# Spreading the routing scatters of a graph layer with eight experts over four steps each

## The chip, the cores and the metric

The kernel runs on one core of one Trainium2 chip. The metric is the device time of one execution in microseconds (us), the median of several runs. Lower is better.

## What is computed

One graph layer and one mixture-of-experts layer follow each other on 6250 nodes of 256 numbers each, in float32, with 100000 edges that are sorted by their target node.

```python
h = layernorm(x)
msg_sum = segment_sum(h[src], dst, N)                 # 100000 edges
agg = msg_sum / maximum(deg, 1)[:, None]
x = x + concatenate([h, agg], axis=1) @ W.T + b       # W is 256 x 512
xn = layernorm(layernorm(x)) * gamma + beta
top_vals, top_idx = top_k(xn @ Wr + br, 2)            # 8 experts, 2 for each node
w = softmax(top_vals)
y = sum over the 2 experts e of w_e * (gelu(xn @ W1[e] + b1[e]) @ W2[e] + b2[e])   # 256 -> 512 -> 256
out = x + y
```

## The kernel before

All engines run one common schedule of numbered steps t, each engine as its own instruction stream; nothing but semaphores ties the streams together. A line such as `if t == ...` in an engine's stream function puts work behind a step of that engine.

**Edge steps, t = 0 to 829.** A step sums 128 edges. GpSimd (POOL) gathers the 128 source rows from `h_rows` in HBM by an indirect DMA (L662). TensorE (PE) multiplies them with a one-hot matrix into a PSUM bank (L764), VectorE (DVE) adds the 257 columns to the node tile's sums in `acc` (L1125). The first 96 steps use 48 gathers twice over, so there are 782 gathers. From step 96 on gather and step go one to one. The gathered rows lie in a ring of `RING` = 17 places, so POOL may be up to 17 steps ahead: it waits for `summed` of step t - 17 (L660).

**Node tiles.** The 49 tiles of 128 nodes close one after another, about every 15 steps. Some steps after a tile has closed, its sums are scaled (ACT L580), transposed and multiplied with W (PE L770, L772, L777, L778), added to x and normalised (DVE L1135 on, ACT L604).

**Batches and routing.** Node tiles are routed in 12 batches (`SIZES = [6, 6, 6, 5, 5, 5, 4, 2, 5, 3, 1, 1]`, `FLUSH = 7`). For batch b the choice of experts is made at `CHOICE[b]`, the places in the experts' queues at `PLACES[b]` (DVE, up to L1040), and the list of expert tiles at `LISTS[b]`. From step `SCATTER[b]`, 17 steps after `PLACES[b]`, POOL scatters the normalised rows from `pay` into `queue` in HBM by 2 * size(b) indirect DMAs (L673), 12 for the first three batches, 10 for the next three, 8 for the seventh, one behind the gather of each step. `pay` and `place_i` have two halves, so batch b + 2 waits for the scatters of batch b (L601, L1039).

**Expert tiles.** 112 tiles of 128 queue rows are computed: SyncE (SP) fetches the rows 6 steps ahead (L540), for a batch's first tile after all scatters of the batch have landed (L533). PE transposes them (L845), ACT copies the expert's W1 into `w1_now` (L625) and the rows (L627), PE makes the hidden layer (L833), ACT the gelu (L633), PE the second product (L858), DVE adds the bias (L1183), and SP stores the result in `answers` (L546). `w1_now` exists once, so a copy waits for the hidden layer of the tile before (L623). The tiles' steps are laid out by hand:

```python
t = SCATTER[b] + 2 * size(b) + 7 if SCATTER[b] < STEPS else max(PLACES[b] + 8, STEPS + 5)
for j in range(UPTO[b], UPTO[b + 1]):
    if begin_at:
        t = max(t, begin_at[-1] + (PACE if begin_at[-1] + PACE < STEPS else 3))
    begin_at.append(STEPS if STEPS - CLEAR <= t < STEPS else t)
```

With `PACE = 7` a tile starts every 7 steps while edge steps run, and every 3 steps afterwards. The first four tiles (batch 0) start at steps 238 to 259, the tiles of batch 1 at 328 to 405, of batch 2 at 418 to 495; from there the tiles follow each other every 7 steps up to tile 74 at step 824. 37 tiles (75 to 111) start at step 830 or later.

**Tail, t = 830 to 976.** The remaining tiles, and `BACK`: each node tile's two answers per node are gathered from `answers` (POOL L685, two per node tile), weighted and added (DVE L1186, L1187) and stored (SP L550). The first 39 node tiles begin 4 steps after tile 84 is done, at step 868, one every two steps; the last 10 wait for the last tile.

Of the kernel before, what the change touches and what calls it, by code (L numbers as in the profile page):

```python
# [48 lines left out]
def build(nc, x, src, dst, gnn_w, gnn_b, gamma, beta, wr, br, w1, b1, w2, b2, out):  # L49
# [14 lines left out]
    STEPS = ET + NT - 1  # L64
# [37 lines left out]
    NB = len(BATCHES)  # L102
    FLUSH = 7
# [240 lines left out]
    def gathered(t):  # L344

        return t - SHARED if t >= BOTH else t // 2 if t % 2 == 0 else None

    def place_of(g):

        return early[:, g, :] if g < SHARED + EXTRA else grow[:, (g - SHARED - EXTRA) % RING, :]  # L350
# [14 lines left out]
    def size(b):  # L365
        return BATCHES[b][1] - BATCHES[b][0]
# [7 lines left out]
    PLACES = [t + 3 for t in CHOICE]  # L374
    LISTS = [t + 1 for t in PLACES]
    SCATTER = [t + AHEAD + 2 for t in PLACES]
    SCATTER = [t if t < STEPS else max(p + 1, STEPS) for t, p in zip(SCATTER, PLACES)]
    begin_at = []
    for b in range(NB):
        t = SCATTER[b] + 2 * size(b) + 7 if SCATTER[b] < STEPS else max(PLACES[b] + 8, STEPS + 5)  # L380
        for j in range(UPTO[b], UPTO[b + 1]):
            if begin_at:
                t = max(t, begin_at[-1] + (PACE if begin_at[-1] + PACE < STEPS else 3))
            begin_at.append(STEPS if STEPS - CLEAR <= t < STEPS else t)
# [12 lines left out]
    def backs(t):  # L397

        return [r for r in range(NT) if BACK[r] == t]

    def back(r, s):

        return grow[:, place_in_ring(STEPS - RING + 2 * (r % PAIRS) + s), 0:D]
# [4 lines left out]
    def answered(engine, j):  # L408

        if j >= 0:  # L410
            engine.wait_ge(s_answer, 16 * (j + 1))
# [239 lines left out]
    def gpsimd_stream():  # L651
        pool.wait_ge(s_hst, 16 * NLB)
        srcs_up.wait(pool)
        for t in range(END):
            g = gathered(t) if t < STEPS else None
            if g is not None:
                if g >= RING:
                    pool.wait_ge(got[g % RING], 16 * (g // RING))
                if g >= SHARED + EXTRA + RING:
                    summed.wait(pool, t - RING)  # L660
                cell_of = CELLS + g if g < SHARED else t
                pool.indirect_dma_start(place_of(g)[:, 0:D], None, h_rows,  # L662
                                        bass.IndirectOffsetOnAxis(srcs[:, cell_of:cell_of + 1], 0)).then_inc(got[g % RING], 16)
            for b in range(NB):
                for n in range(2 * size(b)):
                    if t == SCATTER[b] + n:
                        if n == 0:
                            place_up.wait(pool, b)
                            if b == FLUSH + 1:
                                pool.wait_ge(s_pad, 16 * (X + 1))  # L670
                            if b == NB - 1:
                                pool.wait_ge(s_pad, 16 * (2 * X + 1))
                        pool.indirect_dma_start(queue, bass.IndirectOffsetOnAxis(place_i[:, b % 2, n % 2, n // 2:n // 2 + 1], 0),  # L673
                                                pay[:, b % 2, n // 2, :], None).then_inc(s_sent[b], 16)
            for r in backs(t):
                if r == 0:
                    answered(pool, FIRST_TILES - 1)
                if r == CUT:
                    answered(pool, ALL_TILES - 1)
                if r < PAIRS:  # L680
                    summed.wait(pool, STEPS - RING + 2 * r + 1)
                whole_up.wait(pool, r - PAIRS)
                answer_up.wait(pool, r)
                for s in range(2):
                    pool.indirect_dma_start(back(r, s), None, answers[r >= CUT],  # L685
                                            bass.IndirectOffsetOnAxis(answer_i[:, s, r:r + 1], 0)).then_inc(s_pair[r % PAIRS], 16)
# [507 lines left out]
    sync_stream()  # L1194
    scalar_stream()
    gpsimd_stream()
    tensor_stream()
    vector_stream()
# [24 lines left out]
```

## Time and profile before

| | |
|---|---|
| median of 3 runs | 1425.81 us |
| runs | 1423.88 to 1431.27 us |
| profiled execution, first to last instruction | 1787.5 us |
| granted TensorE clock in it, mean | 0.842 of full |

The profiled execution is 361.7 us longer than the median; no time of its own beside this span is shown for it. The profile says for each engine when it ran an instruction, how long that took, and what ended the idle time before it: the name of a line is what wrote the semaphore, "issue" is time for which the profile shows no wait, and "remote" or "another core or an unknown queue" is a wait whose releaser isn't recorded. A semaphore update can come later than the modelled end of the matmul that sends it. Busy time is not the same as time on the path that sets the end.

### The profile page before, as it was taken

Reading aid. Unit: us, or ns where it says so; the run is one execution under the profiler, and the core shown is the slowest. Engines: PE = TensorE matmul, PEld = TensorE weight load, DVE = VectorE, ACT = ScalarE, POOL = GpSimd, SP = SyncE. Lnnn points to the kernel's source line nnn. Section 1 sums busy time; section 2 is a strip of 40 time slices with the busy share of each in tenths; the row PEclk is TensorE's granted clock in tenths of the full one; section 3 lists DMA queues with packets and bytes.
Section 4 is the critical chain, followed back from the end, with each engine's and each line's share of the span. In section 5 each row is a group of like instructions: output and inputs, shape, how many; then the busy total and the mean of one; then the engine's idle time right before and its main releaser. Section 6 shows DMA issues by size and latency. Waiting matters only on the chain.

```text
span 1787.5 us, 23229 instructions
## 1 busy us (share of the span) xinstructions
PE 1241.8 (69%) x5751; PEld 942.1 (53%) x5751; DVE 812.6 (45%) x2587; ACT 463.2 (26%) x1019; POOL 948.0 (53%) x995
## 2 busy tenths in 40 slices
PE   3223777765874778678787688688788868795881
PEld 2101343442652556556566566566666656684771
DVE  8312663452444445344434444445366565642333
ACT  4200000210220134124124224233322413463440
POOL 3574035666556655655655655665556565115544
PEclk9855998777886889898888889888889889997886
DMA  9732044433333333343333333343344333324553
GB/s 335 247 104 64 1 153 151 133 99 100 110 99 94 107 111 106 115 121 95 113 111 101 110 112 104 109 122 101 115 128 120 105 109 107 101 78 132 160 159 119
DMA packets 128488, 212.63 MB, mean 119 GB/s; under 512 B 25378, under 2 KB 94295, under 8 KB 128119
## 3 DMA queue, kind: packets, MB, share of 16 engines
q0 software_dynamic: 48352, 129.18, 25.2%
q1 hardware_dynamic: 77561, 81.17, 13.7%
q8 instruction: 52, 0.85, 0.2%
q10 hardware_dynamic: 2446, 0.80, 0.2%
q14 instruction: 77, 0.63, 0.1%
HBM read 167.37 MB, written 50.87 MB: 122 GB/s over the span
## 4 chain that ended last, share of the span: by engine, by line
PE 44%; another core or an unknown queue 17%; issue 16%; DVE 11%; ACT 6%; DVEq 2%; DMA 2%; POOL 1%; ACTq 0%; POOLq 0%
PE psum L764 16%; PE psum L833 9%; PE psum L858 8%; DVE acc L1125 5%; PE psum L777 4%; ACT expert_buf L633 2%; PE psum L812 2%; PE psum L778 1%; ACT expert_buf L625 1%; PE psum L845 1%; ACT region L570 1%; DVEq L1118 1%; PE psum L806 1%; PE psum L789 1%
## 5 line engine op out<-in xcount | busy, mean ns | idle before, releaser
L662 POOL DMA_INDIRECT work<-h_rows,srcs x719 | 681.0, 947 | 576.3 <-PE psum L764 324.0
L1125 DVE TENSOR_TENSOR acc<-acc,psum 128x257 f32 x830 | 350.3, 422 | 713.5 <-PE psum L764 329.1
L764 PE MATMUL psum<-work 128*128 128x257 f32 x1438 | 483.6, 450 | 193.7 <-DVE acc L1125 121.9
L764 PEld LDWEIGHTS psum<-work 128*128 128x128 f32 x1438 | 274.7, 219 | 300.3 <-issue 279.1
L833 PE MATMUL psum<-expert_buf 128*128 128x128 f32 x1792 | 235.3, 288 | 40.5 <-ACT expert_buf L625 34.3
L833 PEld LDWEIGHTS psum<-expert_buf 128*128 128x128 f32 x1792 | 230.3, 203 | 50.4 <-ACT expert_buf L625 36.7
L858 PE MATMUL psum<-region,expert_buf 128*128 x896 | 244.7, 422 | 11.6 <-issue 6.5
L633 ACT ACTIVATE expert_buf<-psum,b_col 128x128 f32<-128x128 f32 x448 | 127.8, 370 | 429.7 <-remote 220.0
L858 PEld LDWEIGHTS psum<-region,expert_buf 128*128 128x128 f32 x896 | 186.2, 216 | 49.9 <-issue 21.6
L764 PE MATMUL psum<-region,work 128*128 (+1 forms) x222 | 81.2, 486 | 106.0 <-issue 67.0
L999 DVE TENSOR_TENSOR work<-psum,rel 128x1152 f32<-128x1152 f32 x98 | 126.3, 1289 | 53.6 <-issue 36.7
L685 POOL DMA_INDIRECT work<-answers,answer_i x98 | 93.0, 949 | 108.2 <-DMA answers<-expert_buf 43.5
L625 ACT COPY expert_buf<-region 128x1024 f32 x112 | 117.6, 1050 | 108.7 <-remote 48.2
L673 POOL DMA_INDIRECT queue<-pay,place_i x98 | 97.4, 994 | 85.9 <-DVE place_i L1040 57.7
L580 ACT ACTIVATE acc<-acc,rdeg 128x256 f32<-128x256 f32 x49 | 25.1, 513 | 363.1 <-DVE rdeg L1131 229.5
L777 PE MATMUL psum<-wgt,pair_t 128*128 128x256 f32 x392 | 106.2, 419 | 17.2 <-ACT pair_t L584 11.4
L764 PEld LDWEIGHTS psum<-region,work 128*128 128x128 f32 x222 | 40.8, 220 | 146.0 <-issue 144.0
L1183 DVE TENSOR_TENSOR expert_buf<-psum,b_bc 128x256 f32<-128x256 f32 x112 | 47.2, 422 | 128.2 <-PE psum L858 59.2
L777 PEld LDWEIGHTS psum<-wgt,pair_t 128*128 128x128 f32 x392 | 82.8, 214 | 36.1 <-ACT pair_t L584 15.1
L662 POOL DMA_INDIRECT region<-h_rows,srcs x63 | 59.6, 946 | 35.0 <-issue 18.9
L627 ACT COPY expert_buf<-psum 128x256 f32<-128x256 f32 x112 | 41.6, 371 | 84.8 <-PE psum L845 48.6
L812 PEld LDWEIGHTS psum<-wr_sb,xn_t 128*128 128x128 f32 x196 | 34.6, 242 | 34.8 <-ACT xn_t L610 19.0
(248 smaller groups left out, 896.3 us busy)
## 6 DMA issues: line engine op xcount, KB each, us to landing
expert_buf<-queue SPq DMA_DIRECT2D x112, 128.0 KB
answers<-expert_buf SPq DMA_DIRECT2D x112, 128.0 KB
work<-h_rows,srcs POOLq DMA_INDIRECT x719
region<-in_L_ffn_W_dram SPq DMA_DIRECT2D x16, 512.0 KB
h_rows<-region SPq DMA_DIRECT2D x7, 896.0 KB
own<-h_rows SPq DMA_DIRECT2D x49, 128.0 KB
own<-x_rows SPq DMA_DIRECT2D x49, 128.0 KB
out_dram<-acc SPq DMA_DIRECT2D x49, 128.0 KB
```

Source lines behind the costliest of these rows:

```text
L625: w1c_up.up(act.copy(w1_now, w1_sb[:, ds(e, 1), :, :].rearrange("p a c h -> p (a c) h")))
L633: i = act.activation(gel[j % 2][:, k * P:(k + 1) * P], hidden(j)[:, k * P:(k + 1) * P], ACT.Gelu, bias=b1_col[:, ds(e + k * X, 1)])
L662: pool.indirect_dma_start(place_of(g)[:, 0:D], None, h_rows, bass.IndirectOffsetOnAxis(srcs[:, cell_of:cell_of + 1], 0)).then_inc(got[g % ...
L673: pool.indirect_dma_start(queue, bass.IndirectOffsetOnAxis(place_i[:, b % 2, n % 2, n // 2:n // 2 + 1], 0), pay[:, b % 2, n // 2, :], None ...
L685: pool.indirect_dma_start(back(r, s), None, answers[r >= CUT], bass.IndirectOffsetOnAxis(answer_i[:, s, r:r + 1], 0)).then_inc(s_pair[r % ...
L764: summed.up(pe.matmul(STEP_BANKS[t % BANKS][:, 0:GW], hot[:, k, :], rows, start=True, stop=True))
L777: pe.matmul(PAIR[:, 0:D], pair_t[:, c * P:(c + 1) * P], wgt[:, c, :], start=(c == 0), stop=False)
L812: i = pe.matmul(ROUTE[:, D + n * X:D + (n + 1) * X], xn_t[:, c * P:(c + 1) * P], wr_sb[:, c, :], start=(c == 0), stop=(c == DC - 1))
L833: i = pe.matmul(hidden(j)[:, units], w1_now[:, c, units], xt[j % 2][:, c * P:(c + 1) * P], start=(c == 0), stop=(c == DC - 1))
L858: i = pe.matmul(result(j), gel[j % 2][:, k * P:(k + 1) * P], w2_sb[:, ds(e, 1), k, :].rearrange("p a o -> p (a o)"), start=(k == 0), stop= ...
L999: hot_up.up(dve.tensor_tensor(hot[:, k0:k0 + n, :], COUNT[:, 0:P].unsqueeze(1).broadcast_to([P, n, P]), rel[:, first:first + n].unsqueeze( ...
L1125: added.up(dve.tensor_tensor(sums, sums, STEP_BANKS[t % BANKS][:, 0:GW], ALU.add))
```

## The change

The scatters of batches 0 to 5 stand behind every fourth step, those of batch 6 behind every second, and those of batches 7 to 11 behind each step as before. The first scatter of a batch keeps its step. The first expert tile of a batch is laid 7 steps after the last scatter's group, so it moves.

```diff
+    STRIDE = [4 if b < FLUSH - 1 else 2 if b == FLUSH - 1 else 1 for b in range(NB)]
+    assert all(SCATTER[b] + STRIDE[b] * 2 * size(b) <= SCATTER[b + 1] for b in range(NB - 1) if SCATTER[b + 1] < STEPS)
     begin_at = []
     for b in range(NB):
-        t = SCATTER[b] + 2 * size(b) + 7 if SCATTER[b] < STEPS else max(PLACES[b] + 8, STEPS + 5)
+        t = SCATTER[b] + STRIDE[b] * 2 * size(b) + 7 if SCATTER[b] < STEPS else max(PLACES[b] + 8, STEPS + 5)
...
             for b in range(NB):
                 for n in range(2 * size(b)):
-                    if t == SCATTER[b] + n:
+                    if t == SCATTER[b] + STRIDE[b] * n:
```

By this arithmetic tiles 0 to 69 start 36 steps later (batch 0 at 274 to 295, batch 1 at 364 to 441, batch 2 at 454 on), tiles 70 to 74 start at step 830 to 842 instead of 796 to 824, and tiles 75 to 111 start 15 steps later. 42 tiles instead of 37 start at step 830 or later, and the schedule ends at step 991 instead of 976.

## Rows read from the trace of the kernel before

**Rows 1.** The page: span, engines' busy time, granted clock in 40 slices.
```profile
span 1787.5 us, 23229 instructions
PE 1241.8 (69%) x5751; PEld 942.1 (53%) x5751; DVE 812.6 (45%) x2587; ACT 463.2 (26%) x1019; POOL 948.0 (53%) x995
PEclk9855998777886889898888889888889889997886
```

**Rows 2.** The page's chain that ended last, by engine.
```profile
PE 44%; another core or an unknown queue 17%; issue 16%; DVE 11%; ACT 6%; DVEq 2%; DMA 2%; POOL 1%; ACTq 0%; POOLq 0%
```

**Rows 3.** The gathers of line 662: ns min/median/max, first and last start, waiters.
```profile
L662 POOL DMA_INDIRECT work<-h_rows,srcs x719: 940/946/1015, 138.5 to 1513.0; - x180
L662 POOL DMA_INDIRECT region<-h_rows,srcs x63: 942/946/963, 59.7 to 137.2; - x63
...
who waited for it (us, times):
  PE psum L764: 23.9, 3
```

**Rows 4.** The scatters of line 673, in the same columns.
```profile
L673 POOL DMA_INDIRECT queue<-pay,place_i x98: 967/996/1014, 385.9 to 1577.9; - x98
```

**Rows 5.** POOL's timeline in the scatters of batch 1: start, us, idle before.
```profile
544.91 0.99 POOL L673 DMA_INDIRECT queue<-pay,place_i  x1 [0.56 <-DVE place_i L1040]
546.22 0.97 POOL L662 DMA_INDIRECT work<-h_rows,srcs  x1 [0.31 <-issue]
547.49 1.00 POOL L673 DMA_INDIRECT queue<-pay,place_i  x1 [0.30 <-issue]
```

**Rows 6.** POOL's waits over the span: us, times, longest.
```profile
POOL work L662 <- PE psum L764: 324.0, 189, 83.6
POOL work L662 <- issue: 177.8, 494, 4.1
POOL work L662 <- remote: 74.5, 36, 3.1
```

**Rows 7.** The stretch with expert tiles, POOL: length, busy, instructions, clock, DMA.
```profile
609.00:1514.00 905.00, 525.93 (x552) 0.87 0.38 111
```

**Rows 8.** The same stretch, PE.
```profile
609.00:1514.00 905.00, 705.37 (x3426) 0.87 0.38 111
```

**Rows 9.** The same stretch, DVE's adds of line 1125 alone.
```profile
609.00:1514.00 905.00, 205.32 (x487) 0.87 0.38 111
```

**Rows 10.** The same stretch, POOL's scatters of line 673 alone.
```profile
609.00:1514.00 905.00, 63.76 (x64) 0.87 0.38 111
```

**Rows 11.** DVE's timeline at the end of batch 1's scatters, the step's adds.
```profile
570.43 0.42 DVE L1125 TENSOR_TENSOR acc<-acc,psum 128x257 f32 x1 [4.78 <-remote]
...
579.53 0.42 DVE L1125 TENSOR_TENSOR acc<-acc,psum 128x257 f32 x1 [4.47 <-remote]
```

**Rows 12.** Adds of line 1125 in the first steps, windows.
```profile
70.00:170.00 100.00, 9.73 (x23) 0.54 0.37 110
170.00:226.00 56.00, 28.15 (x67) 0.93 0.00 1
```

**Rows 13.** The chain in the tail: start, us, what.
```profile
1612.40 18.39 another core or an unknown queue
...
1645.69 6.05 another core or an unknown queue
```

**Rows 14.** ACT's timeline in the tail, the copies of line 625.
```profile
1639.60 1.04 ACT L625 COPY expert_buf<-region 128x1024 f32 x1 [1.37 <-PE psum L833]
...
1643.33 1.04 ACT L625 COPY expert_buf<-region 128x1024 f32 x1 [1.37 <-PE psum L833]
```

**Rows 15.** PE's timeline in the tail, the work of one expert tile.
```profile
1637.53 1.95 PE L833 MATMUL psum<-expert_buf 128*128 128x128 f32 x16
...
1639.32 0.38 PE L845 MATMUL psum<-ident,expert_buf 128*128 128x128 f32 x2
...
1639.53 1.89 PE L858 MATMUL psum<-region,expert_buf 128*128 x8
```

## The prediction

> **What bounds the kernel now.** I read the page first [rows 1]: no engine is near full, PE has 69% of the span, POOL 53%, and the chain changes engine all the time [rows 2]. So busy shares alone name no bound. Two things have to be set side by side, the schedule of POOL and the difference between the profiled execution (1787.5 us) and the median (1425.8 us).
>
> POOL issues 782 gathers, the first at 59.7 us, the last at 1513.0 us [rows 3], and 88 of the 98 scatters (batches 0 to 8) stand between them [rows 4]. A gather takes 0.95 us and the next instruction follows after 0.30 us, so 1.25 us; a scatter takes 1.00 + 0.30 = 1.30 us; a gather and a scatter together 2.55 us [rows 3 to 5]. In sum 782 x 1.25 + 88 x 1.30 = 1092 us, of 1453 us between first and last gather. The other 361 us are waits, mostly for the ring of 17 places [rows 6].
>
> Where PE had to wait for a gather the trace names it only 3 times, 23.9 us [rows 3]. In the profiled execution POOL is ahead, and PE and what hangs on it set the pace.
>
> That can't hold in the same measure for the timed runs. After the last gather the profile has 1787.5 - 1513.0 = 274.5 us, in which PE, ACT, DVE and SP stand still together once for 18.4 us and four times for about 6 us [rows 13], 42.5 us in all. So the tail is 232 us without these and 274 us with them. The median leaves 1425.8 - 59.7 - 1092 = 274 us for the tail and all of POOL's waits. So POOL waits between 0 and 42 us in a timed run, and is busy for at least 96% of the gather stretch. The profiled execution's surplus of 361.7 us is then mostly stalls that the timed runs don't have.
>
> The stalls have one look. In steps 6 to 23 an add comes every 4.9 to 5.6 us (23 adds in 100 us), then 67 adds in 56 us [rows 12]; at the end of batch 1's scatters the adds again come 4 to 5 us apart, with 4.8 us of wait for something unrecorded [rows 11]. It looks as if scatters slow the steps. I don't take it so: the same spacing stands in the first 100 us, where there is no scatter, and with POOL busy for 96% of the stretch the edge steps could not be four times slower whenever POOL issues without a pause. The Trainium skill (NOTIFIC — the notification-queue block, section 7.1) says that the block which writes profiling records holds its producers back inside rather than lose a record. By that rule the stalls belong to the profiler and the change removes them from the profile only; no run here shows the rule, and the sum doesn't use it.
>
> **The change part by part.**
>
> 1. *The scatters themselves.* None is added or removed; 88 still stand before the last gather, the same 1092 us of POOL. Price 0 where POOL sets the pace.
>
> 2. *Their spreading.* Before, 10 to 12 steps in a row need 2.55 us of POOL; after, four steps need 3 x 1.25 + 2.55 = 6.3 us, 1.58 us a step. PE needs 705.37 us for 487 steps where tiles run, 1.45 us a step at the granted clock of 0.87; POOL needs there (552 - 64) x 1.25 + 64 x 1.30 = 693 us, 1.42 us a step [rows 7 to 10]. The two are nearly even. A burst of 10 costs POOL 25.5 us while PE uses 14.5 us, so it eats 11 us of a lead that can reach 17 x 1.45 = 24.6 us; in the 65 other steps of a batch POOL wins 65 x (1.45 - 1.25) = 13 us. The lead covers the burst, so I take 0 for the smoothing. Its bounds: nothing, and what an empty lead would cost (rival C).
>
> 3. *Fewer tiles under the edge steps.* The stretch without tile work after batch 0 ends at step 364 instead of 328. So 36 steps go at POOL's 1.25 us instead of the pace with tiles. That pace is at least PE's 1.45 us, and at most (693 + 42) / 487 = 1.51 us, when all of POOL's waits lie there. I take the middle, 1.48: 36 x 0.23 = -8.3 us. Bounds: 0, if POOL sets the pace everywhere (the issues stay the same number), and the whole PE work of five tiles, 1.95 + 0.38 + 1.89 = 4.22 us each [rows 15], so -21.1 us, if PE does.
>
> 4. *More tiles in the tail.* Tiles 70 to 74 now start at step 830 or later, where no gather hides them, ahead of tile 84, on which the first answers hang. Nothing else fills these 15 steps: POOL has no gathers left, and the routing of the last batches ends by the same steps as before. In the tail the copies of L625 are 1643.33 - 1639.60 = 3.73 us apart, each waiting for the hidden layer of the tile before [rows 14]. 5 x 3.73 = +18.7 us. Bounds: 4.22 us a tile if PE's work were not overlapped at all, +21.1; 3.73 + 42.5 / 37 = 4.88 with a share of the stalls, +24.4; below, 5 x 3.73 has nothing to hide it.
>
> 5. *Waits that move.* SP takes the first tile's rows 5 steps after the last scatter instead of 2, so it doesn't wait longer. DVE and ACT wait for the scatters of batch b - 2 before they refill its half; the tightest of these is batch 5, whose last scatter moves from step 633 to 660, and ACT needs its half for batch 7 at step 676. POOL issues the scatter ahead of step 660, so the wait is over: 0 us. Were it not, ACT would stand, behind it the gelu, and PE after that; at 1.48 us a step, 16 steps are 24 us of margin. The scatters' first one, which waits for the places, keeps its step. The Trainium skill (DMA: Bandwidth & Descriptors, Rules for kernel authors) advises to issue a DMA early and to wait for it late. The change does the opposite to the scatters; by this rule alone the sum would be +18.7 us, 1444.5 us, with nothing won. Rows 3 agree in so far as PE rarely waits for a gather.
>
> Sum: 0 + 0 - 8.3 + 18.7 + 0 = +10.4 us. In the median 1425.8 + 10.4 = 1436 us. The profiled execution's own sum would be 1787.5 us plus the same and whatever its stalls do: its bursts of batches 0 and 1 have about 10 slow steps together, some 3 us too long each, so its span can well fall by 20 us while the median rises.
>
> **The rivals.**
>
> *A, the forecast: the tail's five tiles outweigh.* +10.4 us, 1436 us. With POOL as the pace everywhere it is +18.7 us, 1444.5 us, with the tail's upper bound 1450 us. For it: POOL's 1092 us fill nearly all of the gather stretch in a timed run, and the tail's spacing is read straight from a row. Own range 1430 to 1448 us.
>
> *B, no change: PE sets the pace wherever tiles run.* Then the five tiles' PE work leaves the edge steps whole, -21.1 + 18.7 = -2.4 us, 1423 us. For it: PE's 1.45 us a step is above POOL's 1.42 us [rows 7 to 9], and the waits of POOL for the ring [rows 6]. Against it: the 36 freed steps can't run faster than 1.25 us.
>
> *C, faster: the bursts starve PE, and the spreading ends that.* If the lead is empty when a burst begins, the 50 scatters of batches 2 to 6 make steps of 2.55 us instead of 1.48: 50 x 1.07 = 53 us. After, it is (6.3 - 5.92) x 42 for batches 2 to 5 and (3.8 - 2.96) x 8 for batch 6, 23 us. The gain of 30 us lies within the 42 us that POOL could wait at most. With the 10.4 us it gives 1425.8 + 10.4 - 30 = 1406 us. It decides from a gain of 10.4 us on, 2.1 us for each of the five batches. For it: the slow adds at the end of the bursts [rows 11], and a clock that falls to half where PE idles (0.54 in the slow steps, 0.93 after them [rows 12]), which would make a starved PE slow for a while longer. Against it: only 3 waits of PE for gathers [rows 3].
>
> *D, slower by a new wait: a half of `pay` comes free too late.* At 24 us of margin it takes a lead of POOL below zero; some 10 us for each of batches 4 to 8, 1480 us. Hardly likely.
>
> **How the numbers follow.** A 0.45, B 0.25, C 0.27, D 0.03. A measurement of this kernel can tell about 0.5%, 7 us, from no change. A gives slower mostly, with a small part within 7 us; B gives the same, now and then faster; C gives faster, with a part within 7 us. So faster 0.28, same 0.28, slower 0.44. The likeliest is A, 1436 us. The range must take in C's 1406 us and A's 1446 us; beyond them are less than 2 in 10.
>
> **What would show it.** In the profile after: the stretch from the last add to the end longer by 15 to 25 us, 42 copies of L625 in it, still 3.73 us apart between stalls; scatters 4 gathers apart; 70 tiles instead of 75 under the edge steps. POOL's issues still 1.25 us apart. Right is step 3 if the adds between 328 and 364 go at POOL's pace. The prediction is wrong if the gather stretch shrinks by far more than 8 us in timed runs, which the profile alone can't tell because of its stalls: a kernel with the tiles' steps of one version and the scatters' of the other would.

## The result and the profile after

The changed kernel takes 1459.41 us (1454.88 to 1462.87, 4 runs) against 1426.24 us (1423.88 to 1431.27, 4 runs) for the kernel before on the same chip: ratio 1.0232, 95% interval 1.0203 to 1.0262. That is 33 us slower. The forecast was 1436 us, at most 1446 us; its sign was right, its size was not. In a second set of runs the changed kernel took 1460.79 us, ratio 1.0242 (1.0196 to 1.0288). One execution of the kernel before beside experiments 1 to 4 took 3700 us; it counts as slow and is left out of their ratios.

The profile of before that stands ahead (1787.5 us) can't be set beside the one of after (1461.5 us): its picture is that of chips on which this kernel is slower in every run (below, experiments 5 to 12). So the kernel before was profiled again on a chip where it takes 1427 us. Lines of the changed kernel past the edit are 2 higher: L764 is L766 there, L1125 is L1127, L625 is L627.

The page of the kernel before, profiled again: span, busy times, granted clock in 40 slices.

```profile
span 1427.3 us, 23229 instructions
...
PE 1146.9 (80%) x5751; PEld 887.5 (62%) x5751; DVE 812.4 (57%) x2587; ACT 462.9 (32%) x1019; POOL 950.6 (67%) x995
...
PE   3177898778867898988898988988898788799990
...
POOL 2477777777777777777767776767676574205776
PEclk9999998789877989999999999999999988999995
```

The same of the changed kernel.

```profile
span 1461.5 us, 23233 instructions
...
PE 1176.5 (80%) x5751; PEld 902.7 (62%) x5751; DVE 813.4 (56%) x2587; ACT 465.3 (32%) x1020; POOL 951.5 (65%) x995
...
PE   3277898777877779889889988988788797899990
...
POOL 2477777677777766777766776767665663104776
PEclk9999998787987689999989999999899888999995
```

PE runs the same 5751 matmuls in both, and needs 29.6 us longer for them; POOL's busy time is the same to 1 us. So the time shows on PE and not on POOL: the same matmuls ran at a lower granted clock, 0.902 against 0.922 in the mean. That the clock is low doesn't say what made it so, and it doesn't measure the loss: the second profile of the changed kernel is as long (1461.3 us) with 21.5 us more of PE than before, at 0.914.

Where it comes up: the time at which the k-th add of L1125 starts (one for each edge step), read from DVE's records, and the tail from the last add (step 829) to the end. (Two executions of one program can differ here by a few us: before, and the kernel of experiment 3, which is the same up to step 790, are 3.1 us apart at step 780.)

| step | before | changed | difference | gained or lost since the row above |
|---|---|---|---|---|
| 240 | 326.2 | 320.6 | -5.6 | -5.6 |
| 405 | 567.0 | 575.6 | +8.6 | +14.2 |
| 510 | 725.0 | 725.6 | +0.6 | -8.0 |
| 555 | 793.5 | 804.6 | +11.1 | +10.5 |
| 780 | 1153.8 | 1164.9 | +11.1 | 0.0 |
| 829 | 1238.0 | 1254.5 | +16.5 | +5.4 |
| end | 1427.3 | 1461.5 | +34.2 | +17.7 |

The tail, with ACT's copies of L625 or L627 in it; first before, then the changed kernel. Columns: window, its length, ACT busy (copies), granted clock, DMA share, GB/s.

```profile
1238.00:1427.30 189.30, 38.66 (x37) 0.91 0.57 169
```

```profile
1254.50:1461.50 207.00, 43.88 (x42) 0.91 0.55 161
```

And ACT's timeline there in the changed kernel.

```profile
1316.36 1.04 ACT L627 COPY expert_buf<-region 128x1024 f32 x1 [1.37 <-PE psum L835]
...
1320.09 1.04 ACT L627 COPY expert_buf<-region 128x1024 f32 x1 [1.37 <-PE psum L835]
...
1323.82 1.04 ACT L627 COPY expert_buf<-region 128x1024 f32 x1 [1.37 <-PE psum L835]
```

42 copies for 37, still 3.73 us apart, each released by the hidden layer of the tile before, as in [rows 14]. This term came out as forecast. The edge stretch did not: it should have become 8.3 us shorter, and the last add comes 16.5 us later.

The steps 328 to 364, first before, then the changed kernel; columns: window, length, busy time (instructions) of PE, PEld, DVE, ACT, POOL, granted clock, DMA share, GB/s.

```profile
451.60:501.40 49.80, 42.99 (x226) 34.02 (x227) 24.30 (x58) 20.97 (x44) 37.73 (x40) 0.96 0.51 148
```

```profile
446.30:500.20 53.90, 40.55 (x104) 23.12 (x105) 22.89 (x55) 6.50 (x12) 40.80 (x44) 0.68 0.41 123
```

Here lay the forecast's gain. The tiles are gone: PE has 104 matmuls in place of 226. It is busy for 40.6 us with them all the same, since the granted clock fell from 0.96 to 0.68, and the stretch is 4.1 us longer instead of 8.3 us shorter.

The lower clock is not what makes it long; POOL is. The same stretch in the kernel of experiment 18, the changed one with batch 1's scatters in a burst:

```profile
451.50:497.90 46.40, 36.60 (x106) 21.02 (x107) 22.98 (x54) 6.50 (x12) 35.13 (x38) 0.76 0.44 128
```

The changed kernel's second profile has nearly this clock, 0.77, and takes 52.9 us. What differs is that seven of batch 1's scatters stand among the gathers of these 36 steps. From the gather of step 328 to that of step 364 POOL needs 54.2 and 54.3 us in the two profiles of the changed kernel, which is 36 x 1.25 + 7 x 1.30 = 54.1, and never idles for more than 0.31 us in it. With batch 1 in a burst it needs 45.0 us, 36 x 1.25. And it needs 45.0 us in the kernel before as well, tiles or not: its gathers ran at their own pace there already, and only the adds fell back behind them, from 6.1 us behind their gather at step 328 to 10.9 us at step 364.

### The profile page after: what moved, and what is told of

It reads as the page before. It is cut to its first block, busy times and chain, and to the rows that moved or that the text cites. A ratio compares the mean times of both kernels' runs of the same rounds, so it can differ in the third digit from the quotient of the medians.

```text
span 1461.5 us, 23233 instructions
## 1 busy us (share of the span) xinstructions
PE 1176.5 (80%) x5751; PEld 902.7 (62%) x5751; DVE 813.4 (56%) x2587; ACT 465.3 (32%) x1020; POOL 951.5 (65%) x995
## 4 chain that ended last, share of the span: by engine, by line
PE 59%; DVE 13%; issue 10%; ACT 6%; DMA 4%; POOL 4%; DVEq 2%; SPq 0%; ACTq 0%; POOLq 0%
PE psum L766 19%; PE psum L860 14%; PE psum L835 13%; PE psum L779 5%; DVE acc L1127 5%; PE psum L814 2%; POOL work L664 2%; PE psum L780 2%; DMA work<-h_rows,srcs 2%; ACT expert_buf L635 2%; POOL work L687 1%; PE psum L847 1%; DVEq L1120 1%; ACT region L572 1%; ACT pay L606 1%
## 5 line engine op out<-in xcount | busy, mean ns | idle before, releaser
L1127 DVE TENSOR_TENSOR acc<-acc,psum 128x257 f32 x830 | 349.9, 422 | 431.1 <-PE psum L766 365.5
L766 PE MATMUL psum<-work 128*128 128x257 f32 x1438 | 465.4, 440 | 95.5 <-DVE acc L1127 76.5
L766 PEld LDWEIGHTS psum<-work 128*128 128x128 f32 x1438 | 267.3, 213 | 201.5 <-issue 137.4
L860 PE MATMUL psum<-region,expert_buf 128*128 x896 | 238.1, 413 | 6.8 <-ACT expert_buf L629 5.5
L835 PEld LDWEIGHTS psum<-expert_buf 128*128 128x128 f32 x1792 | 219.3, 194 | 7.5 <-issue 1.7
L835 PE MATMUL psum<-expert_buf 128*128 128x128 f32 x1792 | 222.6, 278 | 0.7 <-ACT expert_buf L627 0.7
L860 PEld LDWEIGHTS psum<-region,expert_buf 128*128 128x128 f32 x896 | 180.0, 209 | 40.9 <-issue 14.8
L627 ACT COPY expert_buf<-region 128x1024 f32 x112 | 117.5, 1049 | 63.4 <-PE psum L835 59.8
L779 PE MATMUL psum<-wgt,pair_t 128*128 128x256 f32 x392 | 97.8, 395 | 3.5 <-ACT pair_t L586 3.5
L766 PE MATMUL psum<-region,work 128*128 (+1 forms) x222 | 70.6, 446 | 33.7 <-DVE acc L1127 18.6
L779 PEld LDWEIGHTS psum<-wgt,pair_t 128*128 128x128 f32 x392 | 77.7, 200 | 17.7 <-ACT pair_t L586 6.0
L766 PEld LDWEIGHTS psum<-region,work 128*128 128x128 f32 x222 | 38.9, 206 | 65.0 <-issue 62.1
```

The costliest lines, as they stand in the source:

```text
L627: w1c_up.up(act.copy(w1_now, w1_sb[:, ds(e, 1), :, :].rearrange("p a c h -> p (a c) h")))
L766: summed.up(pe.matmul(STEP_BANKS[t % BANKS][:, 0:GW], hot[:, k, :], rows, start=True, stop=True))
L779: pe.matmul(PAIR[:, 0:D], pair_t[:, c * P:(c + 1) * P], wgt[:, c, :], start=(c == 0), stop=False)
L835: i = pe.matmul(hidden(j)[:, units], w1_now[:, c, units], xt[j % 2][:, c * P:(c + 1) * P], start=(c == 0), stop=(c == DC - 1))
L860: i = pe.matmul(result(j), gel[j % 2][:, k * P:(k + 1) * P], w2_sb[:, ds(e, 1), k, :].rearrange("p a o -> p (a o)"), start=(k == 0), stop= ...
L1127: added.up(dve.tensor_tensor(sums, sums, STEP_BANKS[t % BANKS][:, 0:GW], ALU.add))
```

## The experiments

18 runs of 11 kernels. Every kernel was timed in turns with the kernel before on its chip, and the ratio is to that (beside experiments 1 to 4 its median was 1429.3 us). The last add and the tail in the tables are those of one profile each.

**1 to 4: the two parts of the change, and the tail.** First the kernel before again, then late tiles alone:

```diff
-                    if t == SCATTER[b] + STRIDE[b] * n:
+                    if t == SCATTER[b] + n:
```

then the kernel before with only the start of tiles 70 to 74 put behind the edge steps:

```diff
             if begin_at:
                 t = max(t, begin_at[-1] + (PACE if begin_at[-1] + PACE < STEPS else 3))
+            if j == 70:
+                t = STEPS
```

and the change at half its strength:

```diff
-    STRIDE = [4 if b < FLUSH - 1 else 2 if b == FLUSH - 1 else 1 for b in range(NB)]
+    STRIDE = [2 if b < FLUSH else 1 for b in range(NB)]
```

> The kernel before once more, for a profile whose stalls can be compared with those of the changed kernel. If the long stalls of the first profile (span 1787.5 us against a median of 1426 us) belong to that one recording, a new span lies near 1426 us, as the changed kernel's 1461.5 us lies near its own median, and the last add then comes near 1426 - 19 us of missing tail tiles: about 1238 us with a tail of 188 us. If they belong to the kernel, the span is again far above 1426 us. Time: 1426 us.

> Expert tiles laid as in the changed kernel (36 steps later, 42 in the tail), scatters behind every step as before. The predicted account (the tail's tiles +18.7 us, the freed steps -8.3 us, the spreading 0) gives +10 us, or the whole +33 us if the spreading is free and the later tiles cost more than their tail. If the spreading of the scatters costs the missing 23 us, this kernel is near 1436 us. If the later tiles are what costs, it is near 1459 us.

> The kernel before with tiles 70 to 74 laid into the tail, and nothing else moved: 42 tiles in the tail. The account says +18.7 us for the tail minus what the edge steps 796 to 830 win without five tiles. If these steps were bound by PE, they win up to 21 us and the time stays at 1424 us; if POOL's gathers pace them, the time is 1444 us. In the profile the stretch after the last add grows by 15 to 19 us.

> Scatters of the first seven batches behind every second step, tiles following as laid out (10 to 12 steps later than before). The tail has about 39 tiles. If the cost grows with the tiles moved to the tail alone, +6 us (1432 us). If a scatter stream that is spread costs by itself, this has most of that cost already: above +12 us (1438 us). If the bursts were what cost and 4 is too much, it is below 1426 us.

| kernel | us | ratio (95%) | last add | tail |
|---|---|---|---|---|
| before again | 1426.82 | 0.9983 (0.9957 to 1.0009) | 1238.0 | 189.3 |
| late tiles, scatters in bursts | 1451.71 | 1.0157 (1.0112 to 1.0202) | 1244.7 | 206.5 |
| five tiles to the tail | 1435.54 | 1.0040 (1.0021 to 1.0060) | 1225.8 | 208.4 |
| every second step | 1442.35 | 1.0089 (1.0065 to 1.0113) | 1238.0 | 197.4 |

Late tiles alone, with every scatter where it was, give 22 of the 33 us by the ratios. The five tiles lengthen the tail by 16.0 to 19.1 us in the seven profiles with 42 copies, wherever they come from. Taken out of the last edge steps (experiment 3) they give 12.3 us back at the last add; from step 796 on, where they stood, it is 15.3 us (47.3 against 62.6), and the other 3.0 us were lost before, where the two programs are the same. The late tiles give nothing back: their last add is 6.7 us later. The kernel at half strength has 39 copies in its tail, which is 8.1 us longer than with 37; its last add is where it was, but its profile is that of its fastest run (1436.67 us), 5.7 us below its median.

**5 to 12: on chips that say less.** The kernels for the next two questions: before with tiles 0 to 74 one step later and nothing else; late tiles with bursts, 35 steps later in place of 36; the changed kernel with its tiles 35 later; and the changed kernel with batches 0 and 1 in bursts again.

```diff
-        t = SCATTER[b] + 2 * size(b) + 7 if SCATTER[b] < STEPS else ...
+        t = SCATTER[b] + 2 * size(b) + 8 if SCATTER[b] < STEPS else ...
```

```diff
-        t = SCATTER[b] + STRIDE[b] * 2 * size(b) + 7 if SCATTER[b] < STEPS else ...
+        t = SCATTER[b] + STRIDE[b] * 2 * size(b) + 6 if SCATTER[b] < STEPS else ...
```

```diff
-                    if t == SCATTER[b] + STRIDE[b] * n:
+                    if t == SCATTER[b] + (STRIDE[b] if b >= 2 else 1) * n:
```

> The kernel before with tiles 0 to 74 laid one step later and nothing else: scatters behind every step, 37 tiles in the tail. The longer gap and the tail can't act here. Theory place: what a tile's products cover or hold up at a batch's own events (waits of PE for the normalised rows, for the route) depends on how tile steps and batch steps fall, and the 36 steps of the change are 5 x 7 + 1, so this kernel has most of that shift's cost: 6 to 15 us, 1433 to 1441 us. Theory tail and clock: within 3 us of before.

> As the kernel with late tiles and unspread scatters, but the tiles 35 steps later instead of 36, a whole number of tile intervals of 7, so that tiles and batch events fall on each other as before; 42 tiles in the tail. Theory place: the cost falls from 22 us to what the tail leaves, +19 us less 8 to 12 us: 1435 to 1441 us. Theory that lateness itself costs: as before, 1449 us.

> The changed kernel with its tiles 35 steps later instead of 36. Theory place: it loses the 10 to 15 us as well and keeps the tail and the 10 us of the spreading: 1444 to 1450 us. Otherwise 1459 us.

> The changed kernel with the scatters of batches 0 and 1 behind every step again; those of batches 2 to 6 stay spread, the tiles stay where the change has them. In the profiles the changed kernel falls behind the one with late tiles alone between steps 330 and 375, while batch 1's scatters make POOL's steps 1.58 us long under no tile and the clock halves. Theory early: the 10 us of the spreading are due to batches 0 and 1, and this kernel is near 1449 us. Theory everywhere: each spread batch costs, and it is near 1456 us.

The same four again, on a second such chip:

> The changed kernel, with the scatters of batches 0 and 1 alone put back behind every step; their tile steps stay 36 later and batches 2 to 6 stay spread. On a chip where before takes about 1427 us: theory A (the spread of batch 1 costs about 10 us in steps 328 to 405, the spread of the later ones nothing) expects the time of late tiles with every scatter in a burst, 1452 us, ratio 1.016, and steps 328 to 364 at about 46 us. Theory B (every batch's spread costs a little) expects 1458 us or more, ratio 1.022.

> The changed kernel with its tiles one step earlier in the loop (35 later than before in place of 36), scatters spread. On a chip where before takes about 1427 us: theory A (the one odd step sets the tile steps of each cycle of 75 where their pay copies and the batch's events meet badly, and costs what steps 480 to 555 and 780 to 829 lost) expects about 1446 us, ratio 1.014. Theory B (where the tiles stand against the cycle makes no difference) expects 1459 us, ratio 1.023.

> Late tiles, 35 steps later, every scatter behind every step as before. On a chip where before takes about 1427 us: theory A (place against the cycle of 75 steps) expects 1427 + 18.7 (five copies more behind the last add) - 8.3 (35 freed steps) = 1437 us, ratio 1.007. Theory B (late tiles cost the same wherever they stand) expects 1452 us as with 36, ratio 1.016.

> The kernel before with tiles 0 to 74 one step later and nothing else; 37 tiles stay behind the loop. On a chip where before takes about 1427 us: theory A (place against the cycle) expects 1437 to 1441 us, ratio 1.007 to 1.010, with steps 480 to 555 longer by some 5 us or more than in before. Theory B expects 1427 us, ratio 1.000.

On these two chips the kernel before takes 1790.27 us (17 runs) and 1796.24 us (9 runs), all between 1779 and 1800.

| kernel | first chip | second chip |
|---|---|---|
| before, tiles one step later | 1.0087 (1.0049 to 1.0126) | 1.0094 (1.0058 to 1.0131) |
| late 35, bursts | 1.0091 (1.0060 to 1.0122) | 1.0126 (1.0095 to 1.0157) |
| late 35, spread | 1.0071 (1.0048 to 1.0095) | 1.0105 (1.0068 to 1.0142) |
| late 36, 0 and 1 in bursts | 1.0177 (1.0146 to 1.0208) | 1.0221 (1.0182 to 1.0260) |

Late 36 (with batches 2 to 6 spread) is slower there than late 35 by more than the intervals, 1.0177 against 1.0091 and 1.0221 against 1.0126, some 16 us for one step. Before with its tiles one step later loses 16 to 17 us. No cost of the spread shows where the tiles are 35 steps later (the intervals of the second and third line overlap). How large either is without the 360 us of stalls, these chips can't tell.

**13 to 16: on a chip where before takes 1425.95 us.** The changed kernel beside three of these.

> The changed kernel itself, unchanged, beside the three below. On a chip where before takes about 1427 us it should give 1459 us, ratio 1.023, again. On a chip where before takes about 1790 us, theory A (a cost of the spread of batch 1 and of the tiles' place) expects at least the 1.018 to 1.022 of the version with batches 0 and 1 in a burst; theory B (the stalls of that chip cover what the spread costs) expects less, 1.005 to 1.015.

> As before for this kernel (batches 0 and 1 in a burst again, tiles 36 later). On a chip where before takes about 1427 us: theory A (batch 1's spread is the only one that costs) 1452 us, ratio 1.016 to 1.018; theory B (all batches' spread costs a little) 1458 us or more, ratio 1.022.

> As before for this kernel (tiles 35 later, every scatter behind every step). On a chip where before takes about 1427 us: theory A (place of the tile steps against the cycle of 75 steps) 1437 us, ratio 1.007; theory B (late tiles cost the same wherever they stand) 1452 us, ratio 1.016.

> As before for this kernel (tiles 0 to 74 one step later and nothing else). On a chip where before takes about 1427 us: theory A (place) 1437 to 1441 us, ratio 1.007 to 1.010; theory B 1427 us, ratio 1.000.

| kernel | us | ratio (95%) | last add | tail |
|---|---|---|---|---|
| changed, again | 1460.79 | 1.0242 (1.0196 to 1.0288) | 1253.2 | 208.1 |
| late 36, 0 and 1 in bursts | 1451.33 | 1.0196 (1.0144 to 1.0248) | 1242.0 | 205.3 |
| late 35, bursts | 1446.80 | 1.0165 (1.0107 to 1.0223) | 1236.6 | 206.5 |
| before, tiles one step later | 1441.33 | 1.0106 (1.0065 to 1.0148) | 1249.1 | 192.5 |

Two results. With batches 0 and 1 in bursts again the time is that of all batches in bursts (1451.33 and 1451.71 us; their intervals, 1.0144 to 1.0248 and 1.0112 to 1.0202, would hide 6 us), so no cost or gain shows for the spread of batches 2 to 6, and that of batches 0 and 1 costs 9 us by the medians (1458.6 to 1463.8 us with it, 1448.6 to 1459.2 us without, 4 runs each). By the ratios it is 7 us, and these two intervals overlap; the kernel of experiment 2 against the changed one, 1.0112 to 1.0202 against 1.0203 to 1.0262, says the same more clearly. And one step later, without a tile more in the tail or a scatter moved, costs 15 us: theory A held against B. Late 35 fits neither: 1446.8 us where A wanted 1437 and B 1452. It is 4.5 us below late 36 with batches 0 and 1 in bursts, and that difference is inside the intervals here; against late 36 with every batch in a burst (experiment 2) the ratios show none at all, 1.0165 and 1.0157. Only the two chips above tell the two apart.

The same 15 steps, 510 to 525, in five kernels: before; before with tiles one step later; late 35; late 36; changed.

```profile
725.00:746.50 21.50, 20.61 (x124) 17.48 (x124) 10.08 (x28) 11.80 (x25) 12.71 (x14) 1.00 0.38 109
```

```profile
726.50:755.90 29.40, 24.58 (x118) 19.56 (x118) 10.01 (x28) 11.00 (x24) 14.77 (x17) 0.83 0.30 86
```

```profile
724.50:746.10 21.60, 20.71 (x125) 17.67 (x124) 10.05 (x29) 11.81 (x25) 13.07 (x15) 1.00 0.38 108
```

```profile
715.80:744.20 28.40, 24.27 (x118) 19.74 (x118) 9.91 (x28) 11.03 (x24) 18.41 (x20) 0.83 0.37 109
```

```profile
725.60:754.00 28.40, 24.27 (x118) 19.74 (x118) 9.91 (x29) 11.06 (x24) 19.79 (x22) 0.83 0.39 114
```

21.5 and 21.6 us at full clock where the tiles are a whole number of sevens from before (0, 35), 28.4 to 29.4 us at 0.83 where they are one step more (1, 36). The picture isn't exact to the last us: in experiment 3, the same program up to step 790, these steps take 23.1 us at 0.93. Tiles start every 7 steps, so 35 keeps their place against the other work of a step and 36 doesn't. PE's timeline at the start of this stretch says why. Columns: start, us, engine, line and operation, idle before and what ended it. Before:

```profile
724.09 1.99 PE L858 MATMUL psum<-region,expert_buf 128*128 x8 [1.26 <-ACT expert_buf L627]
725.91 0.60 PE L764 MATMUL psum<-work 128*128 128x257 f32 x2
726.36 0.44 PE L806 MATMUL psum<-ident,pay 128*128 128x128 f32 x2
726.63 1.95 PE L833 MATMUL psum<-expert_buf 128*128 128x128 f32 x16
```

Before with tiles one step later:

```profile
727.88 0.69 PE L806 MATMUL psum<-ident,pay 128*128 128x128 f32 x2 [2.74 <-ACT pay L604]
729.25 3.78 PE L858 MATMUL psum<-region,expert_buf 128*128 x8 [0.68 <-issue]
732.83 1.05 PE L764 MATMUL psum<-work 128*128 128x257 f32 x2
733.68 0.54 PE L812 MATMUL psum<-wr_sb,xn_t 128*128 128x8 f32 x4
734.07 2.03 PE L833 MATMUL psum<-expert_buf 128*128 128x128 f32 x16
```

Before, the tile's second layer (L858, 1.99 us) stands ahead of the transpose L806, which needs ACT's `pay`, and the wait for `pay` is over when PE comes to it. One step later L806 stands first, PE has nothing to do for 2.74 us, and then L858 takes 3.78 us for the same 8 matmuls, twice its time: PE fell from 2.4 to 1.2 GHz. The clock is 1.00 up to 726 us and 0.50 from 727 us on, so it fell in the wait. The granted clock in these windows, before and then one step later:

```profile
724.00:728.00 4.00, 3.91 (x25) 3.46 (x26) 2.50 (x7) 2.29 (x5) 3.09 (x4) 1.00 0.55 148
```

```profile
728.00:733.00 5.00, 4.32 (x11) 3.21 (x12) 0.25 (x1) 1.56 (x4) 3.78 (x4) 0.50 0.37 104
```

The wait, longer by 1.5 us than the 1.26 us before, and the 4.0 us by which PE's busy time grew (24.58 against 20.61 us) are most of the 7.9 us. The Trainium skill (TensorE: Matmul & The Clock Gate, HAM oscillation — how this bites in real kernels) says that an idle gap is paid again as a slow start of the next work; these rows agree, 1.8 us of it in L858 alone.

**17 and 18: direction, and which batch.** Before with tiles one step earlier (`+ 6` for `+ 7`), and the changed kernel with only batch 1 in a burst (`STRIDE[b] if b != 1 else 1`).

> The kernel before with tiles 0 to 74 one step earlier and nothing else; 37 tiles stay behind the loop. On a chip where before takes about 1427 us: theory A (what a tile's matmuls stand between in PE's order decides, and one step later cost 15 us) gives no sign in advance: 1415 to 1441 us, ratio away from 1.000 by more than 0.003 either way, and steps 510 to 525 other than 21.5 us. Theory C (one step later costs because the tiles are later, by their inputs and the order on ACT) expects 1420 us or less, ratio 0.996 or less. Theory B (no effect of the place) expects 1427 us.

> The changed kernel with batch 1's scatters alone put back behind every step (batch 0 and batches 2 to 6 spread, tiles 36 later). On a chip where before takes about 1427 us: if the 9 us that the spread of batches 0 and 1 costs belong to batch 1, 1452 us, ratio 1.016 to 1.018; if they belong to batch 0, 1460 us, ratio 1.023; if to both, between.

| kernel | us | ratio (95%) | last add | tail |
|---|---|---|---|---|
| before, tiles one step earlier | 1433.78 | 1.0055 (1.0034 to 1.0077) | 1243.7 | 188.8 |
| changed, batch 1 in a burst | 1459.35 | 1.0231 (1.0201 to 1.0261) | 1248.7 | 206.5 |

One step earlier is slower too, by 8 us, so it isn't lateness that costs: it is the place (theory C falls). Steps 510 to 525 have 2.5 us of it (24.0 against 21.5); where the rest arises wasn't followed. Batch 1 in a burst wins nothing (1459.35 against 1459.41 and 1460.79 us); with batch 0 in a burst as well it is 1451.33 us. So the medians put the loss on batch 0, though the intervals of experiments 14 and 18 overlap (1.0144 to 1.0248, 1.0201 to 1.0261), and my expectation in experiments 9 and 14, which had put it on batch 1 because the two curves part between steps 330 and 375, wasn't borne out. Batch 1's spread does lose some 7 us between steps 328 and 364, as shown above, but by the medians little of it is left at the end. It is no clean split: the runs of experiment 18 go from 1452.93 to 1461.70 us, and by the profiles' last adds (1242.0, 1248.7, 1253.2 us) batch 0 has 6.7 us and batch 1 4.5 us.

What batch 0's spread does, in POOL's timeline with batch 0 in a burst:

```profile
282.20 1.00 POOL L675 DMA_INDIRECT queue<-pay,place_i  x1 [0.31 <-issue]
283.50 0.96 POOL L664 DMA_INDIRECT work<-h_rows,srcs  x1 [0.30 <-issue]
284.77 1.00 POOL L675 DMA_INDIRECT queue<-pay,place_i  x1 [0.30 <-issue]
286.07 0.96 POOL L664 DMA_INDIRECT work<-h_rows,srcs  x1 [0.30 <-issue]
287.34 1.00 POOL L675 DMA_INDIRECT queue<-pay,place_i  x1 [0.30 <-issue]
```

and with batch 0 spread (experiment 18):

```profile
283.27 1.00 POOL L675 DMA_INDIRECT queue<-pay,place_i  x1 [0.30 <-issue]
287.31 0.96 POOL L664 DMA_INDIRECT work<-h_rows,srcs  x1 [3.05 <-PE psum L766]
288.58 0.95 POOL L664 DMA_INDIRECT work<-h_rows,srcs  x1 [0.30 <-PE psum L766]
```

When batch 0's scatters come up, POOL is as far ahead as the ring lets it: step 210's add is 26.7 us behind its gather. In the burst, scatters fill the time in which POOL would wait for a place anyway. Spread, POOL reaches the full ring sooner and stands for 3.05 us, and the scatters left over come when POOL is needed: at step 240 the add is 7.1 us behind its gather, at step 270 4.0 us (6.5 and 3.9 with the burst, whose scatters are all done by then). From there POOL's gathers stay 2.6 to 2.7 us later than with the burst (step 270: 358.0 against 355.4 us; step 330: 448.8 against 446.1). The size is not exact: from the first gather to that of step 270 the three profiles with batch 0 spread need 297.2 to 299.2 us, the seven on such chips with it in a burst behind every step 295.0 to 296.6. So some 2.7 us have a shown cause. The rest, 4.0 of the 6.7 us at the last add, comes up later, in what such a delay meets, and stays open.

No kernel here beats the kernel before.

## Why the prediction was wrong

**The tail (step 4) was right**: +18.7 us forecast, +17.7 and +18.8 us in the two profiles of the changed kernel, 42 copies 3.73 us apart.

**The freed steps (step 3) failed: -8.3 us forecast, nothing gained.** Three things are wrong in it. The size: it put 36 steps at 1.48 us before, from the stretch of [rows 7 to 10], which comes from a profile with stalls. On an undisturbed chip they take 49.8 us, 1.38 us each, and with late tiles 45.7 us, 1.27 us each, POOL's pace as forecast. The gain is 4.1 us, not 8.3. And POOL's 36 gathers take 45.0 us in both kernels, so POOL set its own pace there before the change too, which is the step's own bound of 0. The count: it let these 36 steps go at 1.25 us each, but step 2 spreads seven of batch 1's scatters into them. Where POOL sets the pace each costs its 1.30 us, and the stretch takes 53.9 and 52.9 us in the changed kernel. Steps 1 and 2 had put them at nothing. They are missing ahead of step 328 in return, and what is left of the difference by the gather of step 364 is 2.4 and 5.8 us: 432.6 and 436.0 us after the first gather, against 430.2 with late tiles and bursts. The kind: it took a gain in one stretch as a gain at the last add. For late 35 it grew to 7.4 us by step 375, and then steps 375 to 480 took 165.3 us against 156.2 us, and it was gone. What remains at the last add is 1.4 us. These 6 us are lost there in that profile, at a granted clock of 0.91 against 0.95 in steps 405 to 480; which wait starts it was not tried.

**A term was missing: the place of the tiles.** The sum had no price for moving tiles by a number of steps that isn't a multiple of the 7 between them. Moving them by one costs 15 us by itself (1.0106), in the other direction 8 us (1.0055), and 16 us in the late tiles on the two chips with stalls. On the undisturbed chips it isn't shown for the late tiles. Their profiles have the last add 8.1 us apart (1244.7 against 1236.6), but their ratios are equal, and the two courses cross several times: late 36 is 8.7 us ahead of late 35 at step 510, loses 6.8 us in steps 510 to 525, and is again 8.7 us ahead at step 700. The forecast treated PE's tile work as a quantity to be put somewhere, and not as what fills PE's waits for ACT.

**The spreading (step 2) was put at 0, and no cost shows for batches 2 to 6.** It is 7 to 9 us for batches 0 and 1, by the medians nearly all of it for batch 0. The argument used an average lead of POOL for every batch. Batch 0 is the case that it didn't look at: a full ring when the scatters begin and hardly a lead after them.

**The moved waits (step 5) were right**: no wait for a half of `pay` comes up, and rival D didn't occur.

**The stalls.** The prediction took 361.7 us for stalls that profiling brings in, with a rule of the Trainium skill (NOTIFIC — the notification-queue block, section 7.1) behind it. The runs don't bear this out. On the chips of experiments 5 to 12 the timed runs take 1790 us as well, and on the others a profiled execution is as fast as the median (1427.3 us of span beside 1426.82). So the stalls go with the chip, and are no surplus of the profiled execution over the timed ones. Whether recording has a part in them on such a chip stays open: every timed run here lists a span and a granted clock too, so none is without records. What the prediction drew from the median held all the same: between the first gather (60.7 us) and the last (1204.6 us) lie 1143.9 us, of which POOL's 1092 are 95%; POOL's waits are 52 us, somewhat above the 42 us that it allowed. But the rows that were to price the steps were taken among the stalls.

**The rivals.** A's mechanism, the tail, is half of the loss. B (PE sets the pace under tiles) is half borne out by the five tiles taken out of the last steps: 15.3 us back from step 796 on, 3.1 us each, between 0 (POOL sets the pace) and 4.22 (PE does). C didn't occur. By the gathers' waiters PE waits for them 24 times, 37.3 us, in the kernel before, and 23 times, 31.8 us, in the changed one (its weight loads 44.3 and 50.5 us), so spreading didn't end those waits. The 3 times of [rows 3], on which the prediction leaned against C, say little: the profiles with the stalls give no landing time for these gathers, and put none of the idle time before L764 down to a landing (64 times, 64.2 us, in the kernel before on an undisturbed chip).

In sum, between the profiles: tail +17.7, late tiles +6.7 at the last add, spread of the scatters +9.8 more: +34.2 us, of 1427.3. The forecast had +18.7, -8.3 and 0. Why late tiles lose 6.7 us where they should have won is the part that stays open; the place of the tiles is a cause shown on its own, not its share here.

## What to carry to other kernels

Where one engine's order is written by hand and its waits are filled by another stage's work, a shift of that stage is not free because the amount of work is the same: try it one step both ways first, alone. The burst of batch 0, on an engine that stood before a full ring, cost nothing; the same instructions spread out can fall where the ring is empty. Where a stretch is priced at one engine's pace, count every instruction that the change puts on that engine there: the scatters that step 2 moved are missing from step 3's sum. And before costing anything from a profile, see that its span matches the median; where it doesn't, take another before reading paces from it.

## What the runs showed of the hardware

Chips differ more than kernels here. Of the chips that ran the kernel before, those above with 1790 and 1796 us took 25% longer for it in every run, with the same picture. DVE's adds of L1125 in the first steps, on such a chip (experiment 5, columns: window, length, DVE busy (adds), clock, DMA share, GB/s):

```profile
70.00:170.00 100.00, 9.73 (x23) 0.55 0.37 110
170.00:226.00 56.00, 28.05 (x67) 0.94 0.00 1
```

and in the kernel before on a chip where it takes 1427 us:

```profile
70.00:170.00 100.00, 49.93 (x119) 0.97 0.48 145
170.00:226.00 56.00, 18.76 (x45) 0.94 0.62 195
```

The first is [rows 12] again, to the count of adds: 23 and 67. What makes those chips slow wasn't found.

On one kind of chip a stretch can repeat closely. Steps 510 to 525 take 28.4 us with 24.27 us of PE in four profiles of three kernels that differ only in their scatters (late 36 in bursts, the changed kernel twice, batch 1 in a burst). It is no rule: the same steps take 21.5 us in the kernel before and 23.1 us in experiment 3, which is the same program up to there.
